# Cross attention on one core: the first head's softmax weights turned by VectorE blocks and transfers through HBM, the second head's by TensorE

## What is computed

```python
def _cross_attention(q_in, kv_in, wq, bq, wk, bk, wv, bv, wo, bo, bias_k, bias_v):
    qh = (q_in @ wq + bq).reshape(b, q_len, H, K)          # H = 16 heads, K = 128
    kh = (kv_in @ wk + bk).reshape(b, t, H, K)
    vh = (kv_in @ wv + bv).reshape(b, t, H, K)
    kh = concatenate([kh, bias_k]); vh = concatenate([vh, bias_v])   # one more key
    logits = einsum('bqhk,bthk->bhqt', qh, kh) / sqrt(K)
    weights = softmax(logits)
    ctx = einsum('bhqt,bthk->bqhk', weights, vh).reshape(b, q_len, H * K)
    return ctx @ wo + bo
```

## Time and profile before

| | us |
|---|---|
| median of 3 runs | 3030.16 |
| lowest and highest run | 3028.36, 3033.15 |
| span of the profiled execution (first to last instruction) | 3031.4 |
| TensorE busy in it | 2882.2 (95%) |
| VectorE busy | 1776.7 (59%) |
| ScalarE busy | 1164.0 (38%) |
| GpSimd busy | 535.5 (18%) |
| moved by DMA | 148.50 MB, mean 49 GB/s |

### The profile page before, as it was taken

The page is one execution under the profiler, slowest core; times in us unless marked ns, Lnnn a source line. Parts: engine busy times, 40 slices in busy tenths (PEclk is TensorE's granted clock), DMA queues, the critical chain, the costliest instruction groups (busy, mean ns, idle before and its releaser), DMA issues.

```text
span 3031.4 us, 40873 instructions
## 1 busy us (share of the span) xinstructions
PE 2882.2 (95%) x14864; PEld 2180.5 (72%) x14864; DVE 1776.7 (59%) x2615; ACT 1164.0 (38%) x2537; POOL 535.5 (18%) x373
## 2 busy tenths in 40 slices
PE   5989898997989999999999999999999999999899
PEld 2333333334778888888888878788888888888787
DVE  6989989897765444455444464554444554444644
ACT  3232323222444444444444343344343443433432
POOL 2847667572001000000000010010000000000100
PEclk8989899997999999999999999999999999999999
DMA  4010010111242111111111112121111101110011
GB/s 161 1 29 28 16 41 2 55 42 42 83 150 74 38 55 38 54 34 39 55 38 55 38 35 62 51 75 37 55 38 55 39 32 55 38 55 28 24 53 56
DMA packets 54204, 148.50 MB, mean 49 GB/s; under 512 B 5936, under 2 KB 6960, under 8 KB 53008
## 3 DMA queue, kind: packets, MB, share of 16 engines
q1 hardware_dynamic: 51248, 143.58, 14.3%
q0 software_dynamic: 2880, 3.94, 0.7%
HBM read 130.98 MB, written 12.58 MB: 47 GB/s over the span
## 4 chain that ended last, share of the span: by engine, by line
PE 68%; DVE 2%; ACT 1%; issue 1%; DVEq 0%; ACTq 0%
PE ca_ps L60 19%; PE ca_ps L62 19%; PE ca_ps L61 19%; PE ca_ps L1978 4%; PE ca_ps L1962 4%; PE ca_ps L1970 2%; PE ca_ps L2004 1%; DVE ca_stats L68 0%; DVE ca_ctx_lo L1770 0%; DVE raw L1739 0%; DVE ca_wq_lo L1697 0%; ACT ca_sk L1655 0%; DVE ca_h_lo L1764 0%; ACT L1655 0%; DVE raw L1759 0%
## 5 line engine op out<-in xcount | busy, mean ns | idle before, releaser
L1527 ACT ACTIVATE ca_pr<-ca_ps,ca_nb 128x129 f32<-128x129 f32 x512 | 181.8, 368 | 511.2 <-DVE ca_nb L1722 511.1
L60 PE MATMUL ca_ps<-ca_h_hi,ca_wq_hi 128*128 128x512 f32 x768 | 313.4, 408 | 4.2 <-DVE ca_h_lo L1764 3.7
L1480 POOL TENSOR_TENSOR ca_dv<-ca_bvr 128x256 f32<-128x256 f32 x32 | 23.6, 737 | 1605.0 <-DVE xq L1707 1444.1
L617 DVE TENSOR_TENSOR_SCAN tm_xn<-tm_wd,tm_vb 128x512 f32<-128x512 f32 x256 | 298.5, 1207 | 13.4 <-POOL tm_xf L322 0.8
L62 PE MATMUL ca_ps<-ca_h_hi,ca_wq_lo 128*128 128x512 f32 x768 | 303.5, 395 | 0.0
L61 PE MATMUL ca_ps<-ca_h_lo,ca_wq_hi 128*128 128x512 f32 x768 | 301.2, 392 | 0.0
L60 PE MATMUL ca_ps<-ca_wv_hi,ca_ctx_hi 128*128 128x256 f32 x1024 | 297.4, 290 | 0.0
L62 PE MATMUL ca_ps<-ca_wv_hi,ca_ctx_lo 128*128 128x256 f32 x1024 | 286.9, 280 | 0.0
L61 PE MATMUL ca_ps<-ca_wv_lo,ca_ctx_hi 128*128 128x256 f32 x1024 | 286.8, 280 | 0.0
L60 PE MATMUL ca_ps<-ca_wo_hi,ca_ct_hi 128*128 128x512 f32 x640 | 253.6, 396 | 0.2 <-DVE raw L1739 0.2
L61 PE MATMUL ca_ps<-ca_wo_lo,ca_ct_hi 128*128 128x512 f32 x640 | 252.7, 395 | 0.0
(11 more groups left out here) (234 smaller groups left out, 5943.5 us busy)
## 6 DMA issues: line engine op xcount, KB each, us to landing
ca_sq<-in_wq SPq DMA_DIRECT2D x49, 512.0 KB, 5.5
ca_so<-in_wo SPq DMA_DIRECT2D x48, 512.0 KB, 3.5
ca_sk<-in_wk SPq DMA_DIRECT2D x33, 512.0 KB, 6.6
ca_sv<-in_wv SPq DMA_DIRECT2D x32, 512.0 KB, 3.7
x_dram<-xres SPq DMA_DIRECT2D x8, 1024.0 KB, 4.2
ca_bvr<-in_bvb SPq DMA_DIRECT2D x32, 256.0 KB, 3.9
raw<-in_l0w SPq DMA_DIRECT2D x6, 1024.0 KB, 7.7
xq<-in_x SPq DMA_DIRECT2D x16, 256.0 KB, 3.7
```

Source lines behind the costliest of these rows:

```text
L60: pe.matmul(out, lhs[0], rhs[0], start=first, stop=False)
L617: v.tensor_tensor_scan(state[t % 2][:, d, :], wd[:, g].rearrange("p b t -> p (b t)"), pair[:, d, :], 0.0, ALU.mult, ALU.add).then_inc(scan ...
L1480: gp.tensor_tensor(dv[:], bvr[:, 0, :], bvr[:, 1, :], ALU.subtract).then_inc(dv_ready, 1)
L1527: ins = act.activation(pr[hd][:, b, :], ps[:, BANK_SC + b // 2, o:o + KW], ACT.Exp, bias=nbs[hd][:, b:b + 1], scale=SCALE, accum_out=sms[h ...
```

## The change

Only in `cross_attend`:

- Head 0 of each unit is no longer turned by TensorE. At the end of `normalise(A, 0)` VectorE turns the 32x32 blocks of `pr[0]` into a new tile `pb` (one instruction, semaphore `blocks_ready`). A new function `probs` in SP's program writes `pb` to a scratch tensor in HBM (256 KB, `blocks_out`), waits for it, and reads it back with four transfers of 64 KB into `pT[0]`, 32 partitions each, with the blocks in their new places (`pt_in`). `context(A, 0)` waits for `pt_in` and reads `pT[0]` in pieces of 32 columns.
- Head 1 stays on TensorE; `transpose` and `probs_out` have one call a unit.
- The order on TensorE changes. In `slot` the first half of the values moves ahead of the turning of head 1; the second half is cut in two parts of 12 matmuls, one between the two contexts and one behind; key 0 is cut in two around the scores of head 1. In `passing` and `mlp_turn` only the first turning goes away.
- `attended` no longer waits for both heads' `ct_split` at its start: its first output block waits for head 0, then for head 1.
- On VectorE `row_max(A, 1)` comes right behind `normalise(A, 0)` in `slot`.
- `probs` stands in SP's program ahead of the loads of `sv` (for quad 1) and of `so` (for quad 0).

```diff
@@ -1324,6 +1325,8 @@
         vT = [common["xq"][:, 2 * i:2 * i + 2, :].rearrange("p a (b m) -> p (a b) m", b=2) for i in range(2)]
         pr = [sb("pr%d" % i, [P, 4, KW]) for i in range(2)]
         pT = [common["xres"][:, 2 + i, :] for i in range(2)]
+        pb = sb("pb", [P, 4, 4, TB])
+        pb_dram = nc.dram_tensor("pb_dram", (P, QT), F32, kind="Internal").ap()
         cT = [two("ct%d" % i, [P, QT]) for i in range(2)]
         uT = [two("u%d" % i, [P, QT]) for i in range(2)]
         mxs = [sb("mx%d" % i, [P, 4]) for i in range(2)]
...
@@ -1428,6 +1432,18 @@
                 b = h * HT + quad * 4
                 sp.wait_ge(o_out, 4 * (h * 48 + 46 + quad) + 4)
                 sp.dma_start(out[b:b + 4].rearrange("b t e -> t b e"), xres[h][:, quad * 4:quad * 4 + 4, :]).then_inc(out_done, 16)
+
+            def probs(h, i, quad):
+                A = Unit(h, i // 8, i % 8, quad)
+                sp.wait_ge(blocks_ready, A.n + 1)
+                sp.wait_ge(pt_in, A.n * 64)
+                sp.dma_start(pb_dram, pb[:].rearrange("p j b s -> p (j b s)")).then_inc(blocks_out, 16)
+                if A.n > 0:
+                    sp.wait_ge(pv_full, A.n * 2 - 1)
+                sp.wait_ge(blocks_out, A.n * 16 + 16)
+                for j in range(4):
+                    sp.dma_start(pT[0][TB * j:TB * j + TB, :].rearrange("r (i x) -> r i x", i=4),
+                                 pb_dram.rearrange("(i r) (j x) -> j r i x", i=4, j=4)[j]).then_inc(pt_in, 16)
 
             res_in(0, 0)
             sp.wait_ge(x3_out, NQ * 16 + 16)
...
@@ -1443,6 +1459,8 @@
                         for quad in range(2):
                             sp.wait_ge(c_split, quad + 1)
                             ctx_in(1, quad)
+                    if i > 0:
+                        probs(h, i - 1, 1)
                     if more:
                         sp.wait_ge(wv_split, kv + 1)
                         sp.dma_start(sv[:], io["wv"][(kv + 1) % 16]).then_inc(wv_in, 16)
...
@@ -1452,8 +1470,10 @@
                     sp.dma_start(sq[:], io["wq"][i + 1]).then_inc(wq_in, 16)
                     sp.wait_ge(wk_split, kv + 1)
                     sp.dma_start(sk[:], io["wk"][(kv + 1) % 16]).then_inc(wk_in, 16)
+                    probs(h, i, 0)
                     sp.wait_ge(wo_split, q + 1)
                     sp.dma_start(so[:], io["wo"][i + 1]).then_inc(wo_in, 16)
+                probs(h, 15, 1)
                 if h == 0:
                     sp.wait_ge(c_split, 3)
                     res_in(1, 0)
...
@@ -1528,9 +1548,9 @@
                                          bias=nbs[hd][:, b:b + 1], scale=SCALE, accum_out=sms[hd][:, b:b + 1])
                 ins.then_inc(exp_done, 1)
 
-            def probs_out(A, hd):
-                act.wait_ge(tr_full, A.n * 2 + (hd + 1))
-                act.activation(pT[hd][:], ps[:, BANK_TR, :], ACT.Copy).then_inc(pt_out, 1)
+            def probs_out(A):
+                act.wait_ge(tr_full, A.n + 1)
+                act.activation(pT[1][:], ps[:, BANK_TR, :], ACT.Copy).then_inc(pt_out, 1)
 
             def context_hi(A, hd):
                 act.wait_ge(pv_full, A.n * 2 + (hd + 1))
...
@@ -1601,15 +1620,14 @@
                 else:
                     split_one(wo, so, wo_in, wo_hi, C.wq)
                 key_out(C, 0)
-                probs_out(A, 0)
                 exps(A, 1)
                 query_out(C, 1, BANK_Q)
                 if C.quad == 1:
                     split_q(C.wq + 1, 0)
                 key_out(C, 1)
-                probs_out(A, 1)
                 if C.quad == 1:
                     split_q(C.wq + 1, 1)
+                probs_out(A)
                 context_hi(A, 0)
                 if C.quad == 1:
                     split_one(wk, sk, wk_in, wk_hi, C.wkv + 1)
...
@@ -1727,6 +1743,10 @@
                 v.wait_ge(rs_done, A.n * 2 + (hd + 1))
                 v.tensor_tensor(pr[hd][:, :, 0:L], pr[hd][:, :, 0:L],
                                 rss[hd][:].rearrange("p (a b) -> p a b", b=1).broadcast_to([P, 4, L]), ALU.mult).then_inc(norm_done, 1)
+                if hd == 0:
+                    v.wait_ge(norm_done, A.n * 2 + 1)
+                    v.wait_ge(blocks_out, A.n * 16)
+                    v.transpose(pb[:].rearrange("p j b s -> p b j s"), pr[0][:, :, 0:L].rearrange("p b (j s) -> p b j s", s=TB)).then_inc(blocks_ready, 1)
 
             def context_lo(A, hd):
                 v.wait_ge(ct_hi, A.n * 2 + (hd + 1))
...
@@ -1813,12 +1833,12 @@
             def slot(A, C):
                 row_max(A, 0)
                 normalise(A, 0)
+                row_max(A, 1)
                 if C.quad == 0:
                     key_col(C, 0)
                     split_one(wv, sv, wv_hi, wv_split, C.wkv)
                 else:
                     split_one(wo, so, wo_hi, wo_split, C.wq)
-                row_max(A, 1)
                 normalise(A, 1)
                 if C.quad == 1:
                     split_q(C.wq + 1, 0)
...
@@ -1934,23 +1954,27 @@
                               [t[:, c, C.quad * QT:(C.quad + 1) * QT] for t in h2], c == 0, c == EC - 1)
                 ins.then_inc(q_full, 1)
 
-            def key(C, hd):
-                pe.wait_ge(k_out, C.n * 2 + hd)
-                pe.wait_ge(wk_split, C.wkv + 1)
-                for c in range(EC):
+            def key(C, hd, chunks=range(EC)):
+                if 0 in chunks:
+                    pe.wait_ge(k_out, C.n * 2 + hd)
+                    pe.wait_ge(wk_split, C.wkv + 1)
+                for c in chunks:
                     ins = mm3(pe, ps[:, BANK_K, :], [t[:, c, hd * P:(hd + 1) * P] for t in wk],
                               [t[:, c, C.quad * QT:(C.quad + 1) * QT] for t in c2], c == 0, c == EC - 1)
-                ins.then_inc(k_full, 1)
-
-            def value(C, i, outs):
-                pe.wait_ge(o_out, outs)
-                pe.wait_ge(wv_split, C.wkv + 1)
-                for b in range(2):
+                if EC - 1 in chunks:
+                    ins.then_inc(k_full, 1)
+
+            def value(C, i, outs, parts=(0, 1)):
+                if 0 in parts:
+                    pe.wait_ge(o_out, outs)
+                    pe.wait_ge(wv_split, C.wkv + 1)
+                for b in parts:
                     t0 = C.quad * QT + (i * 2 + b) * L
                     for c in range(EC):
                         ins = mm3(pe, ps[:, BANK_O + i, b * 256:(b + 1) * 256], [t[:, c, t0:t0 + L] for t in c2],
                                   [t[:, c, :] for t in wv], c == 0, c == EC - 1)
-                ins.then_inc(v_full, 1)
+                if 1 in parts:
+                    ins.then_inc(v_full, 1)
 
             def scores(A, hd):
                 pe.wait_ge(q_out, A.n * 2 + (hd + 1))
...
@@ -1963,20 +1987,24 @@
                                     start=True, stop=True)
                 ins.then_inc(sc_full, 1)
 
-            def transpose(A, hd):
-                pe.wait_ge(norm_done, A.n * 2 + (hd + 1))
-                pe.wait_ge(pt_out, A.n * 2 + hd)
+            def transpose(A):
+                pe.wait_ge(norm_done, A.n * 2 + 2)
+                pe.wait_ge(pt_out, A.n)
                 for b in range(4):
-                    ins = pe.transpose(ps[:, BANK_TR, b * L:(b + 1) * L], pr[hd][:, b, 0:L], ident[:])
+                    ins = pe.transpose(ps[:, BANK_TR, b * L:(b + 1) * L], pr[1][:, b, 0:L], ident[:])
                 ins.then_inc(tr_full, 1)
 
             def context(A, hd):
-                pe.wait_ge(pt_out, A.n * 2 + (hd + 1))
+                if hd == 0:
+                    pe.wait_ge(pt_in, A.n * 64 + 64)
+                else:
+                    pe.wait_ge(pt_out, A.n + 1)
                 pe.wait_ge(v_out, A.n * 2 + 2)
                 pe.wait_ge(ct_split, A.n * 2 + hd)
                 for b in range(4):
                     ins = pe.matmul(ps[:, BANK_PV, b * L:(b + 1) * L], vT[A.quad][:, b, hd * P:(hd + 1) * P],
-                                    pT[hd][:, b * L:(b + 1) * L], start=True, stop=True)
+                                    pT[0].rearrange("p (i b s) -> p b i s", i=4, b=4)[:, b] if hd == 0 else pT[1][:, b * L:(b + 1) * L],
+                                    start=True, stop=True)
                 ins.then_inc(pv_full, 1)
 
             def outputs(U, lhs, w, values=None):
...
@@ -1987,12 +2015,13 @@
                     if b > 0 or not (isinstance(U.g, int) and U.o == 0):
                         pe.wait_ge(o_out, U.o * 4 + (b - 1))
                     for k in range(2):
+                        if values is not None and b == 0:
+                            pe.wait_ge(ct_split, U.n * 2 + (k + 1))
                         ins = mm3(pe, ps[:, BANK_O + b % 2, :], [t[:, b * L:(b + 1) * L] for t in lhs[k]],
                                   [t[:, k, :] for t in wo], k == 0, k == 1)
                     ins.then_inc(o_full, 1)
 
             def attended(A, values):
-                pe.wait_ge(ct_split, A.n * 2 + 2)
                 outputs(A, cT, A.wq, values)
 
```

(14 more changed lines are left out.)

16 lines of the change are left out of this document (7 added, 9 removed).

## The result

The changed kernel takes 3047.66 us (median of 4 runs, 3044.03 to 3053.57); the kernel before, run beside it, 3029.26 us (4 runs, 3028.28 to 3033.15). The ratio is 1.0066, with a 95% interval of 1.0054 to 1.0078: slower by 0.7%. The forecast was 3048.0.

The account below looks back on a forecast made before the run. TensorE's own instruction order was taken as the clock. Slots +11.8, passings +4.0, first MLP turn -0.4 and last +2.4 gave +17.8 us: profiled span 3049.2, median 3048.0 us, 8-in-10 range 3022 to 3076.

Parts of the forecast that it names:

- The turning removed: On TensorE, one of two turnings per unit goes: four transposes, 0.44 us, 28 us over 64 units.
- The second context's wait: In each slot, `context(A, 1)` waits for head 0's read-out: new wait 0.65 us, net +0.21, +11.8 us over 56 slots.
- The output product, costed at nothing: In `attended`, 3.0 us of cover against 2.9 to 3.0 needed for head 1's `ct_split`: no wait.
- Slots and the way through HBM, costed at nothing: In slots, 11.6 us between ready weights and first context cover the way, even its upper end of 10.7 us.
- The way itself, 6.6 us: From `normalise(A, 0)` to `context(A, 0)`: block transpose 0.69, write 2.4, issues 1.32, landing 1.9, hand-overs 0.3; ends 6.1 and 10.7.
- The passings, +4.0: In six passings, a 1.1 us wait for the way through HBM, less 0.44: +0.66 us each.
- The MLP turns: First MLP turn: no wait, -0.4 us; last: first context waits for the way through HBM, +2.4 us.
- Rival 1: In slots, the second context goes 2.31 us after the first without waiting, all keep their gain: 3011.6 us; 13%.
- Rival 2: Nothing measurable: a shorter read-out, a wait of 0.35 us a slot, and cheap passings make the terms cancel; 8%.
- Rival 3: Way through HBM at 10.7 us, waits in passings and MLP turns, TensorE's clock may fall: 3080 us; 17% for over 3062.
- Rival 4: `context(A, 0)` reading `pT[0]` in 32-column pieces runs at half pace: 0.8 us a unit, 51 us, 3099 us; 2%.

Follow-up runs that it names:

- hbm_old_order: The changed kernel with the earlier order of a slot put back on TensorE, ScalarE and VectorE, head 0 still through HBM: 3004.00 us, ratio 0.9918.
- two_banks: The changed kernel with head 1's context in the PSUM bank of the turning, so it doesn't wait for head 0's read-out: 3004.27 us, ratio 0.9916.
- order_only: The kernel before with the new slot order and the relaxed wait of `attended`, both heads turned by TensorE, nothing through HBM: 3066.03 us, ratio 1.0123.

## Why the prediction was right, point by point

- **The time.** 3048.0 against 3047.66, in part by luck. The mechanism and the sign are as forecast, but by steps 20.5 us were lost where the sum had 17.8: the slots lost more than forecast (17.4 against 11.8), the passings and the last turn less. The stage before it, whose code is untouched, ended at 918.4 in this profile and between 914.6 and 924.5 over all of them, so a few us of agreement mean nothing.
- **The turning removed.** Costed at 0.44 us; the slots of `hbm_old_order` gained 0.48.
- **The second context's wait.** Right. The forecast was 2.9 to 3.0 us between the contexts and it is 3.00. But its price of 0.65 was the mis-sized term of the slots: with the turning's 0.48 and a net of 0.31, the new order costs 0.79 in a slot (27.04 - 26.25, changed less `hbm_old_order`). The contexts stand 3.00 us apart, and without the wait 2.29 (`two_banks`): 0.71. And a context that has waited is slow to start: the matmul behind it comes 0.88 us after it, where it is 0.81 without a wait (means of 56; the rows above show the 8 matmuls at 1.13 against 1.06), 0.07 more. The list of waits shows 0.56 to 0.57 only. With 0.31 a slot instead of 0.21, the slots gave +17.4, not +11.8.
- **The output product, costed at nothing.** Nearly right in the slots. I had set 3.0 us of cover against a read-out of 2.9 to 3.0 and called it covered. From the first output matmul to the next unit's scores it is 5.61 us in the changed kernel, 5.57 in `hbm_old_order` and 5.64 in `two_banks`: a tie that costs some 0.03 in the changed kernel and 0.07 in `two_banks`. (With 0.71 and 0.07 that is 0.81; some 0.02 goes the other way in the rest of the step.) In the six passings the relaxed wait gains 0.15 each, 0.9 us, which I had at nothing (`order_only`); the changed kernel has the same 2.56 us there from the second context to the output product.
- **Slots and the way through HBM, costed at nothing.** Right, with 5.4 us to spare in the changed kernel; in the old order there would have been 2.6. What my text called the price of the transfers' cover ("what it cost was the cover of the contexts") is what the runs show, and `hbm_old_order` adds that moving the 24 matmuls ahead was not needed.
- **The way itself, 6.6 us.** Where TensorE waited for it in the changed kernel it is 6.1 to 6.3. The block transpose was 0.71 (taken as 0.69); the write landed after 2.0, where I took 2.4 between the rows of 64 and 1024 KB; the reads landed after 1.9 as in the earlier trace rows. By the rule of the Trainium skill (DMA: Bandwidth & Descriptors, Anatomy of one DMA) the two would have been 2.6 and 2.15, as estimates from that page, and the way 7.1. That section states its fit for transfers issued by GpSimd, and SP issued these; carried over to them it is too long, since 2.0 and 1.9 were measured, and the measurement decides.
- **The passings, +4.0.** Measured +1.9 over six. The shorter way makes the wait 0.55 to 0.80 in the four `second`s and nothing in the two turns, instead of 1.1 in each, and the relaxed wait gives 0.15 in each. One wait I missed: in the two turns the value matmuls come earlier by the turning that is gone, and VectorE, which now also turns blocks, has their weights split later; TensorE waits 0.65 and 0.68 us for it (1.3 us in the two, in the list above).
- **The MLP turns.** First -0.5 (I had -0.4), last +1.8 (+2.4, again the shorter way: 11.65 - 9.82 to the first context). In the last one VectorE's 0.71 us also stands in the second softmax's path: from the second scores to head 1's turning it is 2840.86 - 2834.91 = 5.95 us, where it was 2826.92 - 2821.68 = 5.24. It isn't what ends last, since the first context then waits 0.89 us more for the DMA.
- **Rival 1, the read-out does not bite, 3011.6.** It did not happen, but `two_banks` makes it happen by a second bank, and gives 3004.3, 7 us below that case's sum. The price of the passings (+2.1 there instead of +4.0) is 2 us of this; the end of the stage is cheaper too, and part stays open.
- **Rival 2, the terms cancel,** fell with the 3.00 us between the contexts, where it needed 2.66.
- **Rival 3, a long way and a clock fall.** The mean granted clock of the span is 0.979 (before 0.977). The waits of 0.6 us in slots and passings brought no fall: from 1412 to 2400 us the granted clock is 1.00 in both kernels. In the last turn alone there is one, as there was before. The profile in stretches (length, busy time of TensorE, its weight loads, VectorE, ScalarE, GpSimd, granted clock, DMA share, GB/s):

```profile
2836.00:2841.00 5.00, 0.17 (x2) 0.14 (x2) 3.09 (x8) 2.62 (x9) 0.00 (x0) 0.64 0.18 66
2841.00:2845.00 4.00, 3.05 (x12) 2.36 (x12) 2.09 (x5) 1.07 (x3) 1.28 (x2) 0.50 0.60 180
```

  Behind a wait of 4.83 us TensorE goes on at a granted clock of 0.50, the lower of its two levels, and a context takes 2.08 us instead of 1.06.
- **Rival 4, the stride.** From the first context, which reads pieces of 32 columns, to the matmul behind it is 1429.44 - 1428.63 = 0.81 us, before 1426.40 - 1425.59 = 0.81. It costs nothing.
